# Graph layer 1 on one core: the fourth hidden bank's GELU ahead of the first norm on the scalar engine, and the rows turned behind the sixth down chunk

## The reference, cut to what matters

```python
si = x @ attn_w[l, :d]; sj = x @ attn_w[l, d:]
scores = si[:, :, None] + sj[:, None, :] + attn_b[l]
scores = where(scores >= 0, scores, 0.2 * scores); scores = where(mask, scores, -inf)
attn = softmax(scores)
agg = attn @ x
h = layernorm(x + agg, g1[l], beta1[l])            # first norm
ff = gelu(h @ W1[l] + b1[l]) @ W2[l] + b2[l]       # 256 -> 1024 -> 256
x = layernorm(h + ff, g2[l], beta2[l])             # second norm
```

## Time and profile before

| what | value |
|---|---|
| median of 3 runs | 2868.17 us (2867.8 to 2869.59) |
| the profiled execution | 2867.76 us, span 2866.0 us |
| granted TensorE clock over the span | 0.982 |
| PE busy | 2595.1 us, 91% |
| PEld busy | 2381.5 us, 83% |
| DVE busy | 2084.6 us, 73% |
| ACT busy | 1928.5 us, 67% |
| POOL busy | 1669.9 us, 58% |
| graph layers | about 1268 to 2750 us of the span |
| rounds of layer 1, loop part | 1330.5 to 1723.4 us, 25 rounds |

### The profile page before, as it was taken

The page is one execution under the profiler, slowest core; times in us unless marked ns, Lnnn a source line. Parts: engine busy times, 40 slices in busy tenths (PEclk is TensorE's granted clock), DMA queues, the critical chain, the costliest instruction groups (busy, mean ns, idle before and its releaser), DMA issues. The chain is left out here.

```text
span 2866.0 us, 118375 instructions
## 1 busy us (share of the span) xinstructions
PE 2595.1 (91%) x44257; PEld 2381.5 (83%) x44352; DVE 2084.6 (73%) x6935; ACT 1928.5 (67%) x5044; POOL 1669.9 (58%) x2677
## 2 busy tenths in 40 slices
PE   7999999888888888869999999999999999999956
PEld 5777777677777777759999999999999999999945
DVE  7999999834444444448888887877777788888868
ACT  4676666644444444448888888788887778888734
POOL 6777777610000000027888886766766678888845
PEclk9999999999999999979999999999999999999979
DMA  3111111000000000020000011100000100000003
GB/s 100 38 37 37 37 45 37 13 12 13 13 13 13 13 13 13 12 77 27 24 26 27 24 37 45 31 9 9 9 9 9 33 28 7 9 9 9 8 12 106
DMA packets 110839, 74.62 MB, mean 26 GB/s; under 512 B 51504, under 2 KB 109360, under 8 KB 110512
## 3 DMA queue, kind: packets, MB, share of 16 engines
q1 hardware_dynamic: 96800, 61.03, 7.5%
q10 hardware_dynamic: 13968, 12.72, 1.5%
HBM read 51.68 MB, written 22.02 MB: 26 GB/s over the span
## 5 line engine op out<-in xcount | busy, mean ns | idle before, releaser
L1638 PE MATMUL g_H<-g_hT_upper,g_w_upper 128*128 128x256 f32 x1536 | 461.5, 300 | 0.2
L1658 PE MATMUL g_F<-g_w_upper,g_act_upper 128*128 128x256 f32 x1536 | 443.6, 289 | 13.4 <-DVE g_act_rest L1403 12.9
L1638 PE MATMUL g_H<-g_hT_upper,g_w_rest 128*128 128x256 f32 x1536 | 435.1, 283 | 0.0
L1638 PE MATMUL g_H<-g_hT_rest,g_w_upper 128*128 128x256 f32 x1536 | 434.8, 283 | 0.0
L1658 PE MATMUL g_F<-g_w_upper,g_act_rest 128*128 128x256 f32 x1536 | 431.7, 281 | 0.0
L1658 PE MATMUL g_F<-g_w_rest,g_act_upper 128*128 128x256 f32 x1536 | 431.0, 281 | 0.0
L758 POOL COPY l_xt<-seq 128x64 f32 x256 | 60.5, 236 | 599.7 <-PE l_O L769 596.0
L1184 ACT ACTIVATE g_act_raw<-g_H,g_small 128x256 f32<-128x256 f32 x768 | 317.6, 468 | 54.8 <-PE g_H L1638 53.5
L1403 DVE TENSOR_TENSOR g_act_rest<-g_act_raw,g_act_upper 128x512 fp32r<-128x512 f32 x384 | 301.1, 784 | 44.5 <-ACT g_act_upper L1189 37.7
L1658 PEld LDWEIGHTS g_F<-g_w_upper,g_act_upper 128*128 128x128 f32 x1536 | 289.8, 189 | 23.1 <-DVE g_act_rest L1403 23.0
L330 ACT ACTIVATE a_probs<-a_S,a_nmax 128x256 f32<-128x256 f32 x512 | 237.1, 482 | 104.4 <-DVE a_nmax L428 81.3
(11 more groups left out here) (225 smaller groups left out, 8055.2 us busy)
## 6 DMA issues: line engine op xcount, KB each, us to landing
gmask<-masks ACTq DMA_DIRECT2D x97, 128.0 KB, 2.0
x<-in_x_dram SPq DMA_DIRECT2D x32, 256.0 KB, 3.1
a_adj<-in_adj_dram SPq DMA_DIRECT2D x32, 256.0 KB, 2.7
hidden<-l_hs SPq DMA_DIRECT2D x512, 16.0 KB, 1.4
seq<-hidden SPq DMA_DIRECT2D x32, 256.0 KB, 2.7
out_dram<-q_res SPq DMA_DIRECT2D x32, 256.0 KB, 2.1
masks<-gmask SPq DMA_DIRECT2D x32, 128.0 KB, 1.7
g_w_raw<-in_L_gnn_W_dram SPq DMA_DIRECT2D x6, 512.0 KB, 3.9
```

The costliest lines, as they stand in the source:

```text
L1638: last = pe.matmul(hidden_bank[m // 2][:, m % 2 * N:(m % 2 + 1) * N], w[:, c, m * P:(m + 1) * P], x[:, c, :], start=(c == 0 and k == 0), s ...
L1658: last = pe.matmul(ff_bank[:, it * D:(it + 1) * D], x[:, m, it * P:(it + 1) * P], w[:, m, :], start=(m == 0 and it == 0 and k == 0), stop= ...
```

## The change

For layer 1, outside its last round, ACT's queue gets bank 3 ahead of norm1, and PE's queue gets turn_h between down chunks 5 and 6. hT_out stays ahead of warm_up in these rounds; in the other layers and in the crossing round it stays behind it. Nothing is computed otherwise.

```diff
@@ ACT body
-                    early = now[0] == 0 and not crossing
-                    feed(*now, range(2, 3))
-                    if early:
-                        norm1(*ahead)
-                    feed(*now, range(3, NB))
+                    feed(*now, range(2, NB))
                     if crossing:
                         w1_uppers(ahead[0], 0)
-                    if early:
+                    if ahead:
+                        norm1(*ahead)
+                    if ahead and now[0] == 0 and not crossing:
                         hT_out(*ahead)
-                    if ahead and not early:
-                        norm1(*ahead)
                     if soon:
                         warm_up(*soon)
-                    if ahead and not early:
+                    if ahead and (now[0] > 0 or crossing):
                         hT_out(*ahead)
@@ PE body
                     up(*now, range(4, MC))
-                    turning = 4 if now[0] == 0 and ahead[0] == 0 else 6
-                    down(*now, range(0, turning))
+                    down(*now, range(0, 6))
                     if ahead:
                         turn_h(*ahead)
-                    down(*now, range(turning, MC))
+                    down(*now, range(6, MC))
```

## The result

The changed kernel takes 2883.28 us (median of 4 runs, 2881.71 to 2887.18) beside 2867.99 for the kernel before (2865.98 to 2869.59): the ratio is 1.0056, 95% interval 1.0038 to 1.0073. It is slower by 15.3 us. I had forecast 2864.4 and a range of 2860.2 to 2869.0; slower had 0.07. The profiled execution took 2883.4, its span 2881.6, 15.6 more than before.

A forecast was written before the change was run, and what follows sets the result against it. PE was taken to bound the kernel, losing about 1.07 us a loop round at stops. Gains of 25 x 0.10 = 2.5 plus 1.7, less 0.4, made 3.8 us off the median 2868.17: 2864.4, range 2860.2 to 2869.0.

The forecast's parts named there:

- What bounds the kernel: Layer 1 loop rounds: PE's own work is some 14.65 us of 15.72; about 1.07 is lost at two stops.
- The steps from R on: Loop round timed from R, the end of DVE's third split: chunk 4 R+0.06, turning R+1.57, copy R+2.29, sum R+4.88.
- ACT's loop: Loop round through ACT's copy, exponentials, slopes, table load, GELU and DVE's cast (R+8.31): 15.64 us a round.
- both loops: The chains closing a loop round, by DVE 15.60 us and by ACT 15.64; 15.62 taken, a gain of 0.10 a round.
- a held lock: Sign that the forecast is wrong: loop rounds over 15.75 us, from a late exponential or a held DVE/GpSimd lock.
- Graphs 1, 2 and 28: Layer 1 rounds outside the loop: no change, since they stop for the third split as well.
- Graph 0: First round of layer 1: the turning now comes behind the wait for the third split, loss 0.4 us.
- graphs 29 and 30: Layer 1 rounds without an entering graph: both PE stops go, 15.54 to about 14.70 each, gain 1.7 us.
- The fourth: Rival, chance 0.08: in the loop DVE's next-layer products (L1437) meet GpSimd's second addition (L1090); 16.1 a round, 2876.9 us.
- rival 2: In the loop only PE's own loop counts: 15.45 us a round, 2860.2 in all; chance 0.17.
- 3 (15.72): Rival, chance 0.17: no gain in the loop, the copy of the turned rows slightly later; 15.72 a round, 2866.9 us.

The follow-up runs named there:

- wf_split_first: warm_first with DVE's as_neighbour of the entering graph put behind the third split instead of ahead of it; 2838.35 us, ratio 0.9902.
- pool_late: The changed kernel with two unused 128x2 products on GpSimd ahead of the entering graph's addition (L1099); 2867.19 us, ratio 0.9999.
- enter_halves: The changed kernel with the entering graph's GpSimd addition (L1099) as two instructions of 256 columns; 2870.44 us, ratio 1.0014.
- after_split_first: The changed kernel with DVE's as_neighbour of the entering graph behind the third split instead of ahead of it; 2842.35 us, ratio 0.9919.
- gelu_late3: The kernel before with three unused 240-column copies on ACT ahead of bank 0's GELU in layer 1; 2865.33 us, ratio 0.9998.
- pe_only: The kernel before with only PE's new order, rows turned behind the sixth down chunk; 2874.45 us, ratio 1.0026.
- warm_first: The changed kernel with ACT's tiny Exp and its table load ahead of the copy of the turned rows; 2859.92 us, ratio 0.9974.
- gelu_late10: The kernel before with ten unused 64-column copies on ACT ahead of bank 0's GELU in layer 1; 2911.96 us, ratio 1.016.
- gelu_late1: The kernel before with one unused 240-column copy on ACT ahead of bank 0's GELU in layer 1; 2872.35 us, ratio 1.0022.

## Why the prediction was wrong, point by point

- **What bounds the kernel** held: PE's own work of 14.65 a round, with stops worth about 1.07. wf_split_first, without stops, has 14.75.
- **The steps from R on** held within 0.1: chunk 4 at R + 0.06 (1509.76; forecast R + 0.06), the turning at R + 1.58 (R + 1.57), the copy at R + 2.30 (R + 2.29), the next scores at R + 3.48 (R + 3.55), the sum at R + 4.92 (R + 4.88). The fourth split behind GpSimd took 1.22 (1.24). DVE's wait before the split of the turned rows is 0.73 (0.6). ACT's wait before the copy is 2.57, not about 1.5: the norm ends at 1509.43, R - 0.27, and my own numbers would have given that.
- **ACT's loop** was short by 0.15: the slopes start 0.62 behind the second exponential (1514.51 to 1515.13), where I took "some 0.48", the length of one exponential. GELU is at R + 7.58 (1517.28; the sum gave R + 7.43), the cast at R + 8.45 (R + 8.31).
- **The step that failed** is the last of both loops: "From the sum to R is 1515.45-1504.73 = 10.72" and "From the cast to R is 7.33". I carried a stretch of the old round over as if it were a length. It holds a choice of order between DVE and GpSimd, with some 0.17 in hand at the cast (0.35 behind L1042, the edge is at 0.51 to 0.53). The change used 0.28 (0.14 later on DVE, 0.14 earlier on GpSimd). In its place stands: sum to cast 3.53 (3.39), cast to split 0.47 (0.44), split to aggregate 1.73 (0.86), aggregate to R 5.66 (6.03: bank 1's split meets less of GpSimd, 0.67 instead of 0.98). With R to sum of 4.92 that is 16.31, the measured round; the term mis-sized is split to aggregate, by 0.87. pool_late, enter_halves and the two kinds of rounds of after_split_first show that this is the cause, and graphs 1 and 2 of gelu_late3 show it in the kernel before; pe_only and the loop of gelu_late3 show that half of the shift is not enough. The prediction had named loop rounds over 15.75 as a sign of "a held lock", but it put that at nothing for the first split, without a reason.
- **Graphs 1, 2 and 28**, priced at nothing, lost 1.6 and 0.67. In graphs 1 and 2 the split took 1.66 behind L1099; in graph 28, where no graph enters any more, it took 1.10 next to GpSimd's L1074. **Graph 0** (+0.41 for +0.4) and **graphs 29 and 30** (-1.67 for -1.7) came as forecast; their split is held as well (1.26 and 1.10), but PE has the room.
- **The rivals.** The fourth named the right mechanism, a product of DVE that comes second to a GpSimd addition, and nearly the right size (16.1 a round, 2876.9), at the wrong place: L1437 stayed at 0.42, and it was the first split and L1099 that met. I gave it 0.08 because I had looked at one pair of instructions only. Rivals 2 (15.45 a round) and 3 (15.72) did not come true either. What stood against rival 2, that the third split is tied to GpSimd, was right: in wf_split_first that tie is cut, and the round goes from 15.49 to 14.75.
- **The Trainium skill**, "SBUF — State Buffer", section "SBUF: two separate sides", says that whichever of the two engines starts first has the shared port pair for its whole instruction and the other is blocked. The traces agree on both sides of the flip: 1.81 for the split behind L1099, 1.26 behind half of it, and 0.66 for GpSimd's L1044 behind the split. I had quoted this rule in the prediction and used it for the third and fourth splits and in rival 4, never for the first split. On "starts first" the traces disagree at the cast, as far as the start times of the record go: L1042 starts 0.35 ahead of it, yet the cast takes its 0.41 and L1042 0.80 instead of 0.69, ending with the cast; at a distance of 0.50 it takes 0.97. The cast has one input from SBUF and took 1.53 behind L1100. The page names two SBUF inputs or a perf mode with two ports, so only the second could apply to it, which no run here shows.

What stays open: why pool_late has 15.80 and not 15.6; what decides the rounds at the edge (0.51 to 0.53); when exactly the ports are handed over (the split ends 0.56 behind the end of L1099 by its record, and GpSimd's spans are rough); and how exactly the two 0.14 are shared between ACT's copy and the longer slopes step.

## What to carry to other kernels

A stretch taken over from an old trace is a length only if nobody races in it. Before counting on it, list the pairs of DVE and GpSimd instructions that start within a few tenths of each other, with the lead of the one that must come first (0.17 us here, found two instructions ahead of the one that lost), and price the flip (here 1.12 us on the split, 0.6 on the round) wherever the change moves either by as much as the lead. Place the instruction that the slow path waits for ahead of the race, and let the engine with room be the one that is held.

## What the runs showed of the hardware beside that

- Who comes first of two instructions that start 0.01 to 0.03 us apart is worth 0.6 us a round, and adding two operations to GpSimd made the 32 rounds of the layer shorter by 14.5 us (523.9 to 509.4). A 128x2 GpSimd operation of 0.19 to 0.20 takes 0.64 to 0.72 when it comes behind a DVE split.
- Both table loads of ACT took 1.28, and the next instruction started 1.29 to 1.30 behind their start in every kernel here, also where the load was moved into a wait (warm_first, 1512.92).
- PE's pace in later layers differed between kernels whose edits don't touch them: ten rounds of layer 2 took 147.07 us in the kernel before, gelu_late10 and wf_split_first, but 145.49 in gelu_late3, 148.07 in gelu_late1 and 146.67 in pool_late. All three of the latter add tiles in SBUF, and so does gelu_late10. This is why gelu_late3's total is under the kernel before with longer rounds in layer 1 (rounds 0 to 31 of layer 1: 515.8 against 507.7), and gelu_late1's above it. The cause was not tried.
